# A hybrid attention and expert kernel on one core: GpSimd's scatters, final-norm steps and gathers in other places, the second expert group in other PSUM banks beside the rope prologue

## What is computed

```python
x = x + attn_a(layernorm(x))   # 4 layers: ln, causal ALiBi attention (16 heads of 8), ln, FFN 128-512-128; final norm
x = x + moe(layernorm(x))      # 8 experts of 128-512-128, top 2 by hyperbolic distance to centroids
x = x + attn_b(layernorm(x))   # causal attention with rope, 16 heads of 8, one layer
x = x + moe(layernorm(x))      # the same experts again
```

```python
def layer_norm(x, w, b): return (x - mean(x)) * rsqrt(var(x) + 1e-5) * w + b
scores = einsum('bhqd,bhkd->bhqk', q, k) / sqrt(8) + mask        # causal, plus ALiBi in attn_a
out = einsum('bhqk,bhkd->bhqd', softmax(scores), v) @ Wo
top_v, top_i = top_k(-arccosh(arg(x @ Wp + bp, centroids)), 2); top_w = softmax(top_v)
out = sum over the two picked experts e: top_w * (gelu(x @ W1[e] + b1[e]) @ W2[e] + b2[e])
```

## Time and profile before

| | |
|---|---|
| median of 3 runs | 2928.26 us (2924.89 to 2928.74) |
| the profiled execution | 2925.35 us |
| its span, first to last instruction | 2923.6 us |
| busy: PE, VectorE, ScalarE, POOL | 2445.0, 1899.2, 1473.6, 1043.6 us |
| mean granted TensorE clock | 0.923 of full |
| chain that ended last | PE 56%, VectorE 16%, POOL 11%, ScalarE 8% |

### The profile page before, as it was taken

How to read it: one execution, slowest core, us unless ns; L and a number is a source line. 1 busy time by engine, 2 the same in 40 slices (tenths; PEclk the granted TensorE clock), 3 DMA queues, 4 the chain that set the end, 5 groups by cost and what they waited for, 6 DMA issues and landing times.

```text
span 2923.6 us, 51484 instructions
## 1 busy us (share of the span) xinstructions
PE 2445.0 (84%) x19022; PEld 1478.5 (51%) x19022; DVE 1899.2 (65%) x5245; ACT 1473.6 (50%) x2646; POOL 1043.6 (36%) x1257
## 2 busy tenths in 40 slices
PE   3799899899899998999987777779866888887994
PEld 2355555555554554554544444348853444443894
DVE  6777677677777777776777776434237888884312
ACT  0366666666666566566654444444421544455452
POOL 6233233232332232232334443332353344444116
PEclk9699999999999999999999888889976988998997
DMA  4253233233233223222221121036842211212675
GB/s 111 65 152 104 80 94 114 73 98 109 76 98 104 83 92 103 90 91 97 85 64 56 54 63 51 12 103 187 246 129 66 72 60 60 59 52 75 188 229 159
DMA packets 158011, 285.51 MB, mean 98 GB/s; under 512 B 22264, under 2 KB 111992, under 8 KB 156024
## 3 DMA queue, kind: packets, MB, share of 16 engines
q1 hardware_dynamic: 149376, 264.23, 29.6%
q0 software_dynamic: 8384, 17.97, 2.2%
HBM read 227.33 MB, written 95.96 MB: 111 GB/s over the span
## 4 chain that ended last, share of the span: by engine, by line
PE 56%; DVE 16%; POOL 11%; ACT 8%; issue 5%; DMA 2%; SPq 1%; POOLq 0%; ACTq 0%; DVEq 0%
PE bank L547 14%; PE bank L519 8%; PE bank L533 7%; DVE mx L1161 6%; PE bank L610 4%; PE bank L682 4%; PE bank L672 4%; POOL big L1442 3%; PE bank L621 3%; ACT big L763 3%; PE bank L521 3%; POOL xnR L1419 2%; POOL x_rows L1401 2%; PE bank L567 2%; PE bank L582 2%
## 5 line engine op out<-in xcount | busy, mean ns | idle before, releaser
L763 ACT ACTIVATE big<-bank 128x512 f32<-128x512 f32 x1600 | 933.4, 599 | 1010.7 <-PE bank L533 1007.9
L1161 DVE TENSOR_REDUCE mx<-bank 128x4 f32<-128x512 f32 x1600 | 1058.9, 685 | 476.4 <-PE bank L521 470.2
L1442 POOL TENSOR_SCALAR_AFFINE_SELECT big<-big 128x768 f32<-128x768 f32 (+1 forms) x640 | 403.6, 654 | 1157.8 <-ACT big L763 1157.5
L519 PE MATMUL bank<-KS,QS 96*128 96x512 bf16 (+3 forms) x2560 | 711.5, 318 | 119.7 <-DVE mx L1161 72.0
L533 PE MATMUL bank<-QS,KS 99*128 99x512 bf16 (+3 forms) x2560 | 636.7, 311 | 85.3 <-ACT big L763 83.9
L547 PE MATMUL bank<-big,V 128*9 128x512 f32 (+3 forms) x5120 | 483.8, 476 | 75.9 <-POOL big L1442 68.4
L519 PEld LDWEIGHTS bank<-KS,QS 96*128 96x128 bf16 x2560 | 259.3, 101 | 548.5 <-DVE mx L1161 271.1
L521 PE MATMUL bank<-mask_a,ident_b 128*128 128x128 bf16 x2560 | 506.4, 229 | 0.0
L533 PEld LDWEIGHTS bank<-QS,KS 99*128 99x128 bf16 x2560 | 219.1, 101 | 226.3 <-ACT big L763 147.1
L521 PEld LDWEIGHTS bank<-mask_a,ident_b 128*128 128x128 bf16 x2560 | 262.1, 102 | 66.1 <-issue 39.4
L830 ACT ACTIVATE big<-bank,big 128x256 f32<-128x256 f32 x368 | 151.1, 471 | 205.3 <-PE bank L672 205.3
(11 more groups left out here) (210 smaller groups left out, 2729.8 us busy)
## 6 DMA issues: line engine op xcount, KB each, us to landing
big<-e_pack SPq DMA_DIRECT2D x92, 578.0 KB, 4.6
QS<-part_scr SPq DMA_DIRECT2D x480, 96.0 KB
KS<-part_scr SPq DMA_DIRECT2D x480, 96.0 KB
part_scr<-parts SPq DMA_DIRECT2D x80, 384.0 KB, 2.5
x_rows<-in_alibi SPq DMA_DIRECT2D x47, 384.0 KB, 5.0
y_rows<-in_alibi SPq DMA_DIRECT2D x47, 384.0 KB, 5.4
big<-x_rows SPq DMA_DIRECT2D x92, 128.0 KB, 2.5
y_rows<-big SPq DMA_DIRECT2D x92, 128.0 KB, 4.5
```

What stands on the lines that cost most here:

```text
L519: mm(bk[:, col:col + w], Q[0:ROW_MAX, hh, t * P:(t + 1) * P], K[0:ROW_MAX, hh, 0:w], start=True, stop=False)
L763: A(dst, src, ACT.Exp).then_inc(exp_done, 1)
L1161: v.tensor_reduce(dst, src, axis=AX.X, op=ALU.max).then_inc(a_used, 1)
L1442: g.affine_select(out=blocks, in_=blocks, compare_op=ALU.is_ge, fill=0.0, base=0, pattern=[[0, n], [1, P]], channel_multiplier=-1).then_in ...
```

## The change

It does eight things. (1) A stream's scatters in the encoder go from positions 35 to 38 to positions 0 to 3 of the next iteration, but for streams 5 and 7, which stay, one position earlier; in the rope jobs they go from 1 to 4 to 0 to 3. (2) The bias of the final norm is added to the loaded residual an iteration earlier (`final_bias`), so that `final_rows` has two passes; the final-norm and route-norm steps move up a position. (3) `picked_root` goes from 27 to 30 (encoder) and from 37 to 4 of the next iteration (rope), `weights` after it. (4) The causal mask of pass A is added by one matmul a chunk, over one or two blocks of 128 columns, in place of one for each piece: 1600 in place of 2560. (5) The tiles of the second group use bank 4, and 5 with 7, in place of 0, and 1 with 2, and `down` has bank 3 alone, so that it waits for the bias add of the tile just before. (6) The rope prologue runs beside the second group at 3.3 positions a half from q = 9 on, and `finish` comes before the half. (7) Round 0's `gather(0)` is put at q = 0, its combine and the first rope norm at q = 7; the combines of streams 1 to 3 go into the prologue, those of streams 4 to 7 into iterations 0 to 3 of the rope jobs, at position 28, their gathers two DMAs at a time at positions 20 to 23, all four through the buffer `fp_sb`. (8) The clearing of the ALiBi rows is issued at q = 0.

```diff
--- before.py
+++ after.py
@@ -74 @@
-HEAD_LAG = 13
+HEAD_LAG, HEAD_RATE = 8, 3.3
@@ -185 @@
-bankX, bankH, bankY = bank[0], bank[1:3], bank[3:5]
+bankY = bank[3]
+bankX, bankH = [bank[0], bank[4]], [bank[1:3], [bankPV, bankR]]
...
@@ -350 @@
-    for n in range(-2 * CHUNKS + 2 * GTILES[1] - HEAD_LAG, JOBS * CHUNKS):
+    for n in range(JOBS * CHUNKS):
-    for h in range(2 * ETILES):
+    for h in range(2 * GTILES[0]):
-        q = h - 2 * GTILES[0]
-        if q >= 0:
-            finish(round_, q)
-            if head and q >= HEAD_LAG:
-                head(q - HEAD_LAG)
+    n = 0
+    for q in range(2 * GTILES[1]):
+        while head and n < HEAD_RATE * (q - HEAD_LAG):
+            head(n)
+            n += 1
+        finish(round_, q)
+        h = 2 * GTILES[0] + q
+        tile(round_, h // 2, h % 2)
+    while head and n < 2 * CHUNKS:
+        head(n)
+        n += 1
@@ -403 @@
-COMBINE_FROM, COMBINE_EVERY = (HEAD_LAG - 2, 7), 6
-COMBINE = {4: (-2, 25), 5: (-2, 35), 6: (-1, 10), 7: (-1, 20)}
-COMBINE_BESIDE = 4
+COMBINE_FROM, COMBINE_EVERY, COMBINE_BESIDE = 7, 6, (1, 4)
+COMBINE = {1: (-2, 27), 2: (-1, 8), 3: (-1, 28), 4: (0, 28), 5: (1, 28), 6: (2, 28), 7: (3, 28)}
+GATHER = {1: (-2, 15), 2: (-2, 36), 3: (-1, 16), 4: (0, 20), 5: (1, 20), 6: (2, 20), 7: (3, 20)}
+def gather_buffer(S):
+    return 0 if 4 <= S < JOBS else S % 2
+def gathers(S):
+    return sum(gather_buffer(n) == gather_buffer(S) for n in range(S + 1))
+def beside(i):
+    return i >= GTILES[0]
@@ -510 @@
-                    pe.wait_ge(ey_added, ETILES)
+                    pe.wait_ge(ey_added, GTILES[0])
-                   start=True, stop=False)
-                last = mm(bk[:, col + w - P:col + w], ident_b[:], mask_a[:], start=False, stop=True)
+                   start=(n == 0), stop=False)
+            tiles_of_keys = bk[:].rearrange("p (n c) -> p n c", c=P)
+            blocks = tiles_of_keys[:, (3, 2, 3, 2, 1)[k]:TT:(1, 1, 1, 1, 2)[k], :]
+            last = mm(blocks, ident_b[:], mask_a[:].unsqueeze(1).broadcast_to([P, 2 if k in (1, 3, 4) else 1, P]), start=False, stop=True)
+                if j == 0 and rope_job:
+                    pe.wait_ge(ey_added, ETILES)
@@ -660 @@
...
+        if i == GTILES[0]:
+            jobs = ENC + round_ * JOBS
+            pe.wait_ge(slots_ready, JOBS * (round_ + 1))
+            pe.wait_ge(ot_done, QUADS * jobs)
+            pe.wait_ge(x_added, 2 * jobs - 1)
+            pe.wait_ge(f_added, 2 * ENC - 1)
-            mm(bankH[ft // 2][:, (ft % 2) * TILE:(ft % 2 + 1) * TILE], W1[i % DEEP][:, ft * P:(ft + 1) * P],
+            mm(bankH[beside(i)][ft // 2][:, (ft % 2) * TILE:(ft % 2 + 1) * TILE], W1[i % DEEP][:, ft * P:(ft + 1) * P],
-        if n >= 2:
-            pe.wait_ge(ey_added, n - 1)
+        if n >= 1:
+            pe.wait_ge(ey_added, n)
-                last = mm(bankY[n % 2][:, h * D:(h + 1) * D], hT[n % 2][:, ft, h * P:(h + 1) * P],
+                last = mm(bankY[:, h * D:(h + 1) * D], hT[n % 2][:, ft, h * P:(h + 1) * P],
...
@@ -884 @@
-            dve.wait_ge(combined, JOBS)
+            dve.wait_ge(combined, 4)
...
@@ -1241 @@
-                     (places, -1, 38), (weights, -2, 1))
+                     (places, -1, 38), (weights, -2, 7))
-            route = ((route_layernorm, 0), (final_apply, 3), (second_layernorm, 7), (route_apply, 10),
+            route = ((route_layernorm, 0), (final_apply, 2), (second_layernorm, 6), (route_apply, 9),
-                     (picked, 26), (places, 34), (weights, 36))
+                     (picked, 26), (places, 34), (weights, 38))
...
@@ -1268 @@
-        S, at = divmod(q - COMBINE_FROM[round_], COMBINE_EVERY)
-        if at == 0 and 0 <= S < COMBINE_BESIDE:
+        S, at = divmod(q - COMBINE_FROM, COMBINE_EVERY)
+        if at == 0 and 0 <= S < COMBINE_BESIDE[round_]:
-        if round_ == 0 and q == HEAD_LAG - 1:
-            rope_ln()
+            if round_ == 0:
+                rope_ln()
...
@@ -1366 @@
+    def final_bias(M):
+        pool.wait_ge(xr_loaded, 16 * (M + 1))
+        fb = fin_sb[:, D:2 * D].unsqueeze(1).broadcast_to([P, TT, D])
+        g.tensor_tensor(xload, xload, fb, ALU.add).then_inc(xr_biased, 1)
-        fb = fin_sb[:, D:2 * D].unsqueeze(1).broadcast_to([P, TT, D])
-        pool.wait_ge(rfin_step, 4 * M + 1)
+        pool.wait_ge(rfin_step, 3 * M + 1)
-        pool.wait_ge(rfin_step, 4 * M + 2)
-        g.tensor_tensor(rows, rows, fb, ALU.add).then_inc(rfin_step, 1)
-        pool.wait_ge(rfin_step, 4 * M + 3)
-        pool.wait_ge(xr_loaded, 16 * (M + 1))
+        pool.wait_ge(rfin_step, 3 * M + 2)
+        pool.wait_ge(xr_biased, M + 1)
@@ -1402 @@
-    def gather(S):
-        m = S % JOBS
-        if first_of_group(S):
-            for n in range(3):
-                done = S // JOBS * ETILES + (GTILES[0] if m == 0 else ETILES)
-                pool.wait_ge(y_stored[n], 16 * len(range(n, done, 3)))
-        if S >= 2:
-            pool.wait_ge(combined, S - 1)
-        if S % 2 == 1:
-            pool.wait_ge(x_scattered[0], 16 * TT * JOBS * (S // JOBS + 1))
-            pool.wait_ge(x_scattered[1], 16 * TT * JOBS * (S // JOBS + 1))
-        elif S < 2:
-            pool.wait_ge(y_ready, ENC)
-        for c in range(2 * TT):
+    def gather(S, k):
+        buf = gather_buffer(S)
+        if k == 0:
+            if first_of_group(S):
+                for n in range(3):
+                    done = S // JOBS * ETILES + (ETILES if S % JOBS else GTILES[0])
+                    pool.wait_ge(y_stored[n], 16 * len(range(n, done, 3)))
+            if S < 2:
+                pool.wait_ge(y_ready, ENC)
+            for n in range(2 if buf == 1 else 0):
+                pool.wait_ge(x_scattered[n], 16 * TT * JOBS * (S // JOBS + 1))
+            before_it = [n for n in range(S) if gather_buffer(n) == buf]
+            if before_it:
+                pool.wait_ge(combined, before_it[-1] + 1)
+        for c in range(2 * k, 2 * k + 2):
-                out=yg[S % 2][:, c, :], out_offset=None, in_=y_rows,
-                in_offset=bass.IndirectOffsetOnAxis(ap=slots[:, m, c:c + 1], axis=0)).then_inc(y_gathered[S % 2], 16)
+                out=yg[buf][:, c, :], out_offset=None, in_=y_rows,
+                in_offset=bass.IndirectOffsetOnAxis(ap=slots[:, S % JOBS, c:c + 1], axis=0)).then_inc(y_gathered[buf], 16)
@@ -1453 @@
-        def clear_alibi(b, j):
-            if j == 0:
-                pool.wait_ge(x_added, 2 * ENC)
-                for i in range(2):
-                    g.dma_start(QS[i][ROW_ALIBI:ROW_ALIBI + N_ALIBI, :, :], alibi[2]).then_inc(alibi_cleared, 16)
-            route = ((lambda S: route_rsqrt(2 * S), 1), (final_rows, 4), (lambda S: route_rsqrt(2 * S + 1), 8),
-                     (norm_root, 20), (picked_root, 27)) + tuple(
-                         (lambda S, k=k: scatter(S, k), 35 + k) for k in range(TT))
-            extras += [(lambda b, j, what=what: what(j - ROUTE) if j >= ROUTE else None, -2, (pos, 1))
-                       for what, pos in route]
+            route = ((lambda S: route_rsqrt(2 * S), -2, 1), (final_bias, -1, 33), (final_rows, -2, 3),
+                     (lambda S: route_rsqrt(2 * S + 1), -2, 7), (norm_root, -2, 20), (picked_root, -2, 30))
+            for k in range(TT):
+                route += ((lambda S, k=k: scatter(S, k) if S in (STREAMS[0] - 1, JOBS - 1) else None, -2, 34 + k),
+                          (lambda S, k=k: None if S in (STREAMS[0] - 1, JOBS - 1) else scatter(S, k), -3, k))
+            extras += [(lambda b, j, what=what: what(j - ROUTE) if j >= ROUTE else None, rel, (pos, 1))
+                       for what, rel, pos in route]
-            route = ((lambda S: route_rsqrt(JOBS + S), -1, 20), (norm_root, -1, 31), (picked_root, -1, 37)) + tuple(
-                (lambda S, k=k: scatter(S, k), -2, 1 + k) for k in range(TT))
+            route = ((lambda S: route_rsqrt(JOBS + S), -1, 20), (norm_root, -1, 31), (picked_root, -2, 4)) + tuple(
+                (lambda S, k=k: scatter(S, k), -2, k) for k in range(TT))
-            extras += [(clear_alibi, 2, (0, 1))]
-            extras += [(lambda b, j, S=S, i=i: gather(S) if j == i + 2 else None, 2, (pos - 8, 1))
-                       for S, (i, pos) in COMBINE.items()]
+            extras += [(lambda b, j, S=S, i=i, k=k: gather(S, k) if j == i + 2 else None, 2, (pos + k, 1))
+                       for S, (i, pos) in GATHER.items() for k in range(TT)]
-        S, at = divmod(q - COMBINE_FROM[round_], COMBINE_EVERY)
-        if at == 0 and -1 <= S < COMBINE_BESIDE - 1:
-            gather(round_ * JOBS + S + 1)
-        if round_ == 0 and q == HEAD_LAG - 1:
+        if round_ == 0 and q == 0:
+            pool.wait_ge(x_added, 2 * ENC)
+            for i in range(2):
+                g.dma_start(QS[i][ROW_ALIBI:ROW_ALIBI + N_ALIBI, :, :], alibi[2]).then_inc(alibi_cleared, 16)
+        S, at = divmod(q - COMBINE_FROM, COMBINE_EVERY)
```

(9 more changed lines are left out.)

19 lines of the change are left out of this document (10 added, 9 removed).

## The result

The changed kernel takes 2961.59 us, median of 4 runs (2955.67 to 2963.2), the kernel before beside it 2928.5 us (2924.89 to 2931.34). The ratio is 1.011, 95% interval 1.0092 to 1.0128. The forecast was 2881, with a range that ended at 2914. The profiled execution's span is 2960.2 us, against 2923.6 of before: 36.6 us more where 47 us less stood in the sum.

What follows compares the result with a forecast made beforehand. PE bounds plain encoder jobs; in routed jobs no engine is full and the order of waits decides. Terms -24 - 8 - 4 - 36 + 22 + 3 = -47 took 2925.35 to 2878.4, or 2881.3 as median; 8-in-10 range 2850 to 2914.

Steps and rivals of the forecast that it cites:

- Scatters to positions 0 to 3: Encoder: POOL's clear before `pv` no longer waits behind scatters; 4.8 us in five iterations, -24 us, bounds -15 and -32.
- the ten us for half clock: Encoder: PE's half-clock work behind five gaps before `pv`, 2.0 us each, counted as removed by moving the scatters.
- Rival (c): Encoder: moved scatters delay the clears of positions 4 and 9 and the power; both encoder parts 0, 2913 us; chance 0.07.
- Final norm: Encoder, before the output transposes: one POOL pass less and a position earlier, 1.3 us in six iterations, -8 us, bounds 0 and -16.
- Mask: Pass A: 960 fewer weight loads and matmuls, same columns, some 5 ns a pair, -4 us, bounds 0 and -10.
- (d): Mask: each 128-column pair takes its weight load's 0.10 us, so 960 pairs give 46 us, 2839 us; chance 0.03.
- (e): Mask: the 256-column matmul runs at half rate, 103 us more at most, kernel at 2975 us with 90 uncovered; chance 0.06.
- Tiles and prologue: Round 0's second tile group: rope prologue beside tiles, 4.0 us a half, L1170 at 2201 to 2203, -36 us, bounds -20 and -48.
- a sign of being wrong: Prologue: the prediction is wrong if the stacks of job 0 come later than 2153 us on the old scale.
- Gathers and combines in rope iterations 0 to 3: Rope jobs: VectorE waits about 4 us, then works 2.4; 5.5 us in four iterations, +22 us, bounds +8 and +32.
- `picked_root` and `weights`, dismissed in one sentence: Their later places cost 0, as no PE wait stood behind them before; bound 1 us a rope job either way.
- Round 1: Last tiles: PE stops some 7 us longer, but POOL's unbroken gathers set the end; +3 us, bounds 0 and +8.

Runs made afterwards that it cites:

- Experiment 3: Changed kernel with the encoder's moved scatters at positions 10, 12, 15 and 17 in place of 0 to 3; ratio 0.9928 to the kernel before.
- experiment 7: Experiment 3 and experiment 4 edits together, plus gathers of streams 4 to 7 at 35, 36 of the iteration before and 6, 7; ratio 0.982 to the kernel before.
- experiment 8: Experiment 3 and experiment 4 edits together, leaving out round 0's gathers of streams 4 to 7 and three quarters of their combines' work; ratio 0.9768 to kernel before.
- Experiment 9: Experiment 7 plus the prologue's gathers of streams 1 and 3 at positions 1 to 4; 2871.8 us, ratio 0.9809 to kernel before, 0.9788 again.
- Experiment 2: Changed kernel with the encoder's routing steps and scatters back at their old positions, two passes and early bias kept; ratio 1.0081 to the kernel before.
- experiment 1: Kernel before with only the mask added by one matmul a chunk; ratio 0.9969 to the kernel before.
- experiment 5: Changed kernel with gathers of streams 4 to 7 at positions 10, 12, 15, 17 in place of 20 to 23; ratio 1.0036 to the kernel before.
- experiment 4: Changed kernel with the rope jobs' `picked_root`, `weights` and scatters put back where they stood before; ratio 0.9972 to the kernel before.
- experiment 10: Changed kernel with only the gathers of streams 4 to 7 spread: 35, 36 of the iteration before, and 6, 7; ratio 0.9966 to the kernel before.

## Why the prediction was wrong, by its own steps

**Scatters to positions 0 to 3, forecast -24.** The gap before `pv` went as told, 4 us less in a job. The step that failed is what was given back: "VectorE's norm statistics and POOL's `route_rsqrt`" were priced at 1 us, and `final_rows` was left out, though the text put the scatter ahead of it one paragraph later. Four DMAs of 1.26 us ahead of `final_rows` turn VectorE's 1.91 us into 3.71, and PE's two gaps behind it take 2.2 us back. With them went the ten us for half clock: PE falls to 0.50 behind the new gap instead, and its busy time rose by 6.8 us over the stretch. Rival (c), "the gaps only move", given a chance of 0.07 because of `pv`'s slack, is what happened; its path was another than it named. Experiment 3 shows the forecast's own gain behind the final norm: 25.4 us less than in the kernel before on the chips of 2928 (experiments 7 to 9), where the two encoder terms wanted 32.

**Final norm, forecast -8.** Experiment 2 puts it with the mask at about 3 us, on a slower chip. The pass is gone, but in the changed kernel the scatters ahead of `final_rows`, and not its passes, set VectorE's wait.

**Mask, forecast -4.** The sign and the mechanism held, the size was too small: -4.7 to -5.1 by mark 27 alone, which closes 648 of the 960 pairs, so 7 to 8 ns a pair and not 5; the medians of experiment 1 differ by 9. Rivals (d) and (e), the weight load and the half rate, are out. So is the 81 ns a pair that the Trainium skill gives (TensorE: Matmul & The Clock Gate, "Back-to-back issue gap"), by which these 648 pairs would have given an estimated 18 us.

**Tiles and prologue, forecast -36.** Measured -25.8. PE took up after `gather(0)` at 2108.20; 2116 less the encoder's 8.9 is 2107. Pass A came at 2149.20, 5 late against 2144, so the stacks of job 0 came at 2158 on the old scale, which the forecast had named as a sign of being wrong; the combine of stream 1 had waited 7.57 us for its rows before (2141.88). The 40 positions then took 54.9 us, not 48: in the last halves the bias add stands behind a combine that waits 5.34 us for its rows, and PE, which the one `bankY` (costed at 0) makes wait for that bias add, stands 9.33. Experiment 9, with these two gathers earlier, gave back 8.4 of the 10 on the chip of 2928. What one bank costs by itself was not isolated.

**Gathers and combines in rope iterations 0 to 3, forecast +22.** The wait of 4 us was 4.76 to 7.13, 7 us more than told in the four. Two terms were missing. The clears behind the gathers: in experiment 5 the combine's wait was away and the time was not. And `picked_root` and `weights`, dismissed in one sentence because no wait stood there before: that row of before is of a queue in which `picked_root` stood ahead of the scatters. Jobs 4 to 6, which have no gather, are 4.0, 4.6 and 8.8 us longer. Of the 40.6 us missed, that is 17, and experiments 7 and 8 show it to be `weights`, `picked_root` and the scatters, since with these back the same jobs take what they took before. Jobs 2 and 3 by the same rate are 9; the other 15 lie in jobs 0 to 3, where the combines waited longer and the clears piled up. This part of the division is worked out from jobs and not isolated on this chip. On a slower one experiments 4 and 10 give 15 to 17 for `weights` and 14 for the spread, each alone, and 43 for all edits together, waits without a name included. The granted clock in the stretch fell from 0.90 to 0.85, and PE's busy time rose by 18.3 of the 62.6 us; the forecast had no term for it here.

**Round 1, forecast +3.** Measured +8.7, by another mechanism. PE's stop in the tiles came (9.13 us before L710 at 2886.94) and cost nothing, since POOL's 64 gathers set the end. The 8.2 us by which they start later than the stretch's start are the late `weights` once more: 5.99 us of PE before the output transposes at 2691.16, where before there was 0.22. With `weights` back the stretch takes 290.9 and 291.2 us (experiments 7 and 8), as before.

What was forecast right: the mask's sign, the gap before `pv`, PE's return in the prologue to 1 us, and that VectorE would wait in the rope jobs. What was wrong in the encoder and in the rope jobs is a step that stood behind a moved DMA in POOL's queue and was not priced, and half clock that was counted as gone.

## What to carry to other kernels

When DMAs are moved on an engine that also computes, list every instruction behind the new place up to the next idle of that engine, and price each one's waiters at the full length of the run of DMAs (here 10 us for eight), not only at the one you meant to free. Put them where the trace shows the engine idle for at least their length, and split them over several such places: on one chip a rope job took 73.6 us with eight gathers together and 66.0 with them in two fours, with POOL as busy. Don't count the half clock behind a gap as saved with the gap: here it came back behind the next one. That a step has no wait in the trace says something of its old place in the queue, not of the step.

## What the runs showed of the hardware

**A VectorE tensor_scalar waits out GpSimd's passes, but not its DMA issues.** In the changed kernel the four instructions of L917 start at 1734.57 and end at 1738.82, 4.25 us for what takes 1.11 alone (the median of one is 335 ns; the longest, in three of the routed jobs, 3484). These are POOL's rows beside it:

```profile
1734.53 1.14 POOL L1460 TENSOR_TENSOR resid<-qk,parts 128x512 f32<-128x512 f32 x1
1735.63 1.22 POOL L1475 TENSOR_SCALAR_AFFINE_SELECT big<-big 128x768 f32<-128x768 f32 x2
1736.83 1.14 POOL L1465 TENSOR_TENSOR parts<-resid,parts 128x512 bf16<-128x512 f32 x1
```

VectorE finishes 0.85 us after POOL's last of them, which is time for three short ones: one instruction stood for nearly the whole run of POOL's work. L906 beside the scatters kept its 0.34 us (at most 0.51 in 32). The Trainium skill (SBUF — State Buffer, "Who interferes with whom") has a tensor_scalar in a two-port mode and GpSimd lock each other out; the trace agrees for passes, and shows no lock for DMA issues, so the 1.5 us each that the prediction set beside it for `final_apply` did not come.

**Chips differ by 3% on this kernel**, with mark 27 of the kernel before equal to the tenth of a us and the same bytes moved at 168 and 128 GB/s in the last stage, and the same change cost 33 us on one and 5 to 8 on others.

**On the slower chips VectorE stands for PE's result beside a run of indirect DMAs.** Each of 222 waits of over 2 us that the profile can put down to nothing lies beside them, in twelve traces; on the chips of 2928 us there is none in five. Beside eight DMAs together they reach 6.5 us in a rope job, and with the gathers in fours and the scatters back those that are left take 2.3 to 3.7. Why is open.

**An indirect DMA costs POOL 1.26 us** where it has nothing to wait for (0.95 busy and 0.30 to the next): that is the median from one to the next in each of the seventeen traces.
